# A fused attention and mixture-of-experts layer, its repeated step put into another order on all four engines

## The chip, the cores and the metric

One core of a Trainium2 chip runs the whole kernel. The metric is the device time of one execution in microseconds (us). A core has four compute engines with a queue each, worked through strictly in order: TensorE (PE in the profile, with PEld for its weight loads), VectorE (DVE), ScalarE (ACT) and GpSimd (POOL). SyncE (SP) issues transfers. Engines meet only at semaphores: an instruction that waits holds up everything behind it in its own queue.

## The reference

The input x has 16 sequences of 256 tokens with 128 features. Per token it is layer-normalised to xn, and the output is x plus an attention of xn plus a mixture of experts of xn:

```python
# attention, per sequence
x_tran  = xn @ W + b
weights = exp(tanh((x_tran @ xn.T) * (1 / |i - j|)))     # diagonal set to zero
attn    = (weights / (sum(weights, -1) + 1e-7)) @ xn
# experts: 8 of them, hidden size 176, each token takes its best 2
scores = sigmoid(xn @ gate_w.T); sel = top2(scores + expert_bias)
routed = sum over sel of relu((xn * score) @ w_up.T)**2 @ w_down.T      # bf16
shared = relu(xn @ shared_w_up.T)**2 @ shared_w_down.T                  # f32, hidden 176
y = x + attn + routed + shared
```

## The kernel before, in words

Two sequences make a chunk: 4 tiles of 128 tokens. There are 8 chunks (`NCH` = 8, `LAST` = 7). A chunk goes through three stages, and at each moment three chunks are under way: in iteration `k` of the repeated step, `f = k` is in its front, `c = k - 1` in its middle, `o = k - 2` in its end. The loop runs `k` = 3 to 7 (five steps). Chunks 0 to 2 are started by a list written out by hand before it, and a written-out tail follows it.

On TensorE the pieces are these functions, each with a line number that the profile shows:

- `transpose_x` (L877): the four tiles of xn are transposed into the PSUM bank `small`; ScalarE's `take_xT` (L418) copies them out as xnT.
- `rest` (L893): 64 output rows that hold the 8 gate logits and the last 48 shared hidden units. It writes `small` again, so it waits for `take_xT`. ScalarE reads it twice: `exp_logits` (L429), `relu_rest` (L434).
- `transpose_exp` (L902): the exponentials turned to one token per partition; it waits for both of these reads. VectorE's `route_one` (L641), `route_scores` (L650), `route_bias` (L659), `route_top` (L665), ScalarE's `take_pair`, VectorE's `route_mark` (L672) and GpSimd's `make_gates` (L287, L290) make the gates from it.
- `project` (L921) and `dots` (L936, for q = 0 and 1): xn W, copied by ScalarE's `take_proj` (L453), then its product with xn. VectorE's `weigh` (L686) multiplies by the decay, ScalarE does `take_tanh` and `take_exp` (L457, L462), GpSimd's `mask` (L309) clears the diagonal.
- `attend` (L957, q = 0 and 1): both write the bank `side`. So `attend(c, 1)` waits until ScalarE's `scale_attention` (L475) has read the first; that itself needs VectorE's `attend_sums` and `attend_norm` (L723, L727).
- `shared_main` (L970), `shared_down_rest` (L1011, with 64 rows of weights), `shared_down_main` (L1017): the shared expert. GpSimd squares its two hidden parts (`square_shared`, `square_rest`).
- `up_tile(c, t)` (L980, three matmuls, one per PSUM bank of `h_ps`) makes 1408 hidden values for each of 128 tokens. There is one such set of banks. VectorE's `gate(c, t)` (L698) reads it and multiplies by the gates; only when it has ended may the next `up_tile` start (semaphore `h_taken`). ScalarE's `square` (L505) follows, then SyncE turns the result by a transfer (L213), and `down_tile(c, t)` (L1029, eleven matmuls) takes it.

VectorE's `finish(c, h)` (L751) adds two tiles of the result, and SyncE stores them. `norm_stats` (L608, L616) on VectorE, then `rsqrt` and `normalize` (L263 to L276) on GpSimd make xn of a coming chunk, four tiles one after the other.

The order on every engine is only the order in which these calls are written. In the step before, TensorE runs up(c,0), attend(c,0), shared_down_rest(o), rest(f), up(c,1), shared_down_main(o), down(o,2), transpose_exp(f), attend(c,1), project(f), up(c,2), shared_main(c), dots(f,0), down(o,3), up(c,3), transpose_x(f+1), dots(f,1), down(c,0), down(c,1). The tail begins with `up_by_bank(0)` (L984 to L998), which is an `up_tile` of the last chunk whose two halves are gated separately, and waits in the same way for `gate(6, 3)`.

Of the kernel before, what the change touches and what calls it, by code (L numbers as in the profile page):

```python
# [12 lines left out]
P = 128  # L13
D = 128
# [17 lines left out]
def moe_attention_kernel(nc, x, early, late, up, down, out):  # L32
    NCH = x.shape[0]

    with ExitStack() as ctx:
# [129 lines left out]
        LAST = NCH - 1  # L165

# [83 lines left out]
        def _(pool):  # L250
# [127 lines left out]
            for k in range(3, NCH + 1):  # L378
                f, c = k, k - 1
                add_x(c)  # L380
                if f < NCH:
                    square_rest(f)
                if k + 1 < NCH:
                    rsqrt(k + 1)
                if k + 1 < NCH:
                    normalize(k + 1)
                if f < NCH:
                    make_gates(f)
                square_shared(c)
                if f < NCH:  # L390
                    mask(f, 0)
                if f < NCH:
                    mask(f, 1)
                if k + 1 < NCH:
                    narrow(k + 1)

        @block.scalar
        def _(act):
# [179 lines left out]
        def _(dve):  # L578
# [231 lines left out]
            finish(0, 0)  # L810
            gate(1, 3)
            finish(0, 1)
            weigh(2, 1)
            for k in range(3, NCH):
                f, c, o, g = k, k - 1, k - 2, k + 1
                gate(c, 0)
                attend_sums(c, 0)
                attend_norm(c, 0)
                if g < NCH:
                    norm_stats(g)  # L820
                gate(c, 1)
# [12 lines left out]
                finish(o, 1)  # L834
                weigh(f, 1)
# [21 lines left out]
        def _(pe):  # L857
            t_ = nc.tensor

            def transpose_x(c):  # L860
                if c == 0:
                    pe.wait_ge(ident_made, 1)
                if c == 1:
                    pe.wait_ge(rest_taken, 1)
                elif c == 2:
                    pe.wait_ge(expT_taken, 2)
                elif c > 2:
                    pe.wait_ge(proj_taken, c)
                for t in range(TILES):
                    if c == 0 and t < TILES - 1:  # L870
                        pe.wait_ge(first_xn_ready, t + 1)
                    elif c == 0:
                        pe.wait_ge(fourth_xn_ready, 1)
                    else:
                        pe.wait_ge(second_xn_ready, t - 1) if c == 1 and t > 1 else pe.wait_ge(xn_ready, xns(c, t))
                    bank, at = (dots_ps, t * P - S) if c == 0 and t >= 2 else (small, t * P)
                    last = t_.transpose(bank[:, at:at + P], xn[:, c, t, 0:D], ident[:, :])  # L877
                    if c == 0 and t == 1:
                        last.then_inc(first_half_made, 1)
# [310 lines left out]
```

## Time and profile before

| | before |
|---|---|
| median of 3 runs | 118.19 us (117.75 to 118.61) |
| the profiled execution, span from first to last instruction | 116.0 us |
| TensorE busy | 110.6 us (95%) |
| VectorE busy | 101.1 us (87%) |
| ScalarE busy | 89.5 us (77%) |
| GpSimd busy | 69.6 us (60%) |
| granted TensorE clock | 1.000 in every slice |

For the profiled execution only its span is given; the time of a run, as its median has it, is 2.2 us longer than that span, which lies around the first and the last instruction. In the profile a matmul of f32 operands is recorded as two instructions. Matmuls overlap: the time from the start of one piece to the start of the next is shorter than the duration shown. The chain of waits cuts the same stretch into pieces that add up.

### The profile page before, as it was taken

What the parts mean: (1) busy time and instruction counts of PE and PEld (TensorE: products, weight loads), DVE (VectorE), ACT (ScalarE), POOL (GpSimd) and SP (SyncE); (2) the same over time, 40 slices, a digit from 0 to 9 for tenths busy, and PEclk for the clock granted to TensorE, in tenths of its full rate; (3) what the DMA queues carried; (4) which work ended last, traced back from release to release, by engine and by line L of the source; (5) the groups of instructions that cost most, each with busy time, mean ns of one, the idle gap of its engine ahead of it and who ended that gap; (6) DMA issues with size and microseconds to landing.
All of it is one profiled execution on the core that took longest, in us unless ns stands there. A gap on an engine that the chain in (4) does not pass through costs nothing.

```text
span 116.0 us, 2804 instructions
## 1 busy us (share of the span) xinstructions
PE 110.6 (95%) x914; PEld 85.1 (73%) x914; DVE 101.1 (87%) x319; ACT 89.5 (77%) x139; POOL 69.6 (60%) x119
## 2 busy tenths in 40 slices
PE   3988999999999999999999999999999999999991
PEld 3965558787868776869578776879588767859790
DVE  6969989999998989989998989988998689989751
ACT  4444799987788987969799687969699687897760
POOL 6538993499999499635973499636972520613200
PEclk9999999999999999999999999999999999999999
DMA  4999105886776759892849939593949648687882
GB/s 97 319 263 331 68 0 100 78 167 126 139 145 108 195 100 193 54 245 48 167 82 220 124 70 179 103 163 79 172 84 219 124 84 164 117 216 136 131 208 90
DMA packets 47965, 16.56 MB, mean 143 GB/s; under 512 B 45008, under 2 KB 45904, under 8 KB 47952
## 3 DMA queue, kind: packets, MB, share of 16 engines
q1 hardware_dynamic: 47376, 15.44, 66.0%
q0 software_dynamic: 288, 0.72, 3.2%
q10 hardware_dynamic: 288, 0.23, 1.0%
q8 instruction: 7, 0.11, 0.4%
q14 instruction: 6, 0.05, 0.1%
HBM read 3.84 MB, written 2.10 MB: 51 GB/s over the span
## 4 chain that ended last, share of the span: by engine, by line
PE 94%; DVE 1%; issue 1%; POOL 1%; ACT 0%; DVEq 0%; POOLq 0%
PE out_ps L1029 16%; PE h_ps L980 15%; PE side L957 12%; PE dots L936 11%; PE out_ps L1017 6%; PE out_ps L1011 4%; PE small L921 4%; PE side L970 4%; PE small L893 4%; PE out_ps L1059 4%; PE small L877 3%; PE h_ps L993 2%; PE small L902 1%; PE side L912 1%; PE side L921 1%
## 5 line engine op out<-in xcount | busy, mean ns | idle before, releaser
L698 DVE SCALAR_TENSOR_TENSOR gated<-h_ps,gates 128x1408 bf16<-128x1408 f32 x28 | 45.2, 1615 | 4.7 <-PE h_ps L980 4.4
L505 ACT ACTIVATE hidden<-gated 128x1408 bf16<-128x1408 bf16 x30 | 41.1, 1378 | 2.6 <-DVE gated L698 1.6
L1029 PE MATMUL out_ps<-downT,hiddenT 128*128 128x128 bf16 x341 | 22.8, 219 | 0.0
L1029 PEld LDWEIGHTS out_ps<-downT,hiddenT 128*128 128x128 bf16 x341 | 20.8, 98 | 2.3 <-issue 0.6
L980 PE MATMUL h_ps<-upT,xnTb 128*128 128x512 bf16 (+1 forms) x84 | 21.3, 362 | 0.0
L276 POOL TENSOR_SCALAR xn<-x_sb,meanvar,rstd 128x128 f32<-128x128 f32 x26 | 20.4, 795 | 0.6
L957 PEld LDWEIGHTS side<-xn,probs 128*128 128x128 f32 x120 | 15.1, 191 | 1.5 <-issue 0.5
L957 PE MATMUL side<-xn,probs 128*128 128x129 f32 x120 | 15.8, 274 | 0.0
L936 PE MATMUL dots<-projT,xnT 128*128 128x256 f32 x60 | 15.4, 379 | 0.0
L309 POOL TENSOR_SCALAR_AFFINE_SELECT probs<-probs 128x256 f32<-128x256 f32 x16 | 6.5, 408 | 12.7 <-ACT probs L462 12.6
L980 PEld LDWEIGHTS h_ps<-upT,xnTb 128*128 128x128 bf16 x84 | 7.2, 98 | 9.4 <-issue 3.2
L936 PEld LDWEIGHTS dots<-projT,xnT 128*128 128x128 f32 x60 | 10.8, 190 | 3.9 <-issue 1.7
L457 ACT ACTIVATE weighted<-weighted 128x512 f32<-128x512 f32 x16 | 9.9, 620 | 1.9 <-DVE weighted L686 1.9
L686 DVE TENSOR_TENSOR weighted<-dots,decay 128x512 f32<-128x512 f32 x15 | 10.3, 684 | 0.4 <-PE dots L936 0.2
L321 POOL TENSOR_TENSOR resid<-scaled,x_sb 128x256 f32<-128x256 f32 x8 | 5.8, 729 | 7.5 <-ACT scaled L475 7.5
L315 POOL TENSOR_TENSOR shidden<-srelu 128x512 f32<-128x512 f32 x8 | 8.3, 1039 | 3.3 <-ACT srelu L467 3.3
L462 ACT ACTIVATE probs<-weighted 128x512 f32<-128x512 f32 x16 | 10.0, 625 | 0.3
L1017 PEld LDWEIGHTS out_ps<-late_sb,shidden 128*128 128x128 f32 x62 | 7.8, 191 | 1.0
L1017 PE MATMUL out_ps<-late_sb,shidden 128*128 128x128 f32 x62 | 8.4, 278 | 0.0
L271 POOL TENSOR_TENSOR rstd<-var_eps,minus_half 128x4 f32<-128x4 f32 x7 | 7.3, 1041 | 0.6
L713 DVE SCALAR_TENSOR_TENSOR gated<-h_ps,gates 128x704 bf16<-128x704 f32 x8 | 6.8, 886 | 0.5 <-PE h_ps L993 0.4
L429 ACT ACTIVATE expneg<-small,gate_sign 128x256 f32<-128x256 f32 x8 | 3.8, 474 | 4.4 <-PE small L893 4.3
(117 smaller groups left out, 178.9 us busy)
## 6 DMA issues: line engine op xcount, KB each, us to landing
x_sb<-in_x SPq DMA_DIRECT2D x7, 256.0 KB, 9.1
out_y<-final SPq DMA_DIRECT2D x7, 256.0 KB, 2.5
hiddenT<-hidden SPq DMA_TRANSPOSE x31, 3.6
upT<-in_up POOLq DMA_DIRECT2D x1, 352.0 KB, 7.5
downT<-in_down POOLq DMA_DIRECT2D x1, 352.0 KB, 8.4
late_sb<-in_late SPq DMA_DIRECT2D x1, 192.0 KB, 3.6
x_sb<-in_x ACTq DMA_DIRECT2D x1, 128.0 KB, 2.4
x_sb<-in_x SPq DMA_DIRECT2D x1, 128.0 KB, 2.5
```

The costliest lines, as they stand in the source:

```text
L276: g.tensor_scalar(xn[:, c, t, 0:D], x_sb[:, c, t, :], meanvar[:, c % 2, t, 0:1], rstd[:, c % 2, t:t + 1], ALU.subtract, ALU.mult).then_inc ...
L315: g.tensor_tensor(shidden[:, c % 2, :], srelu[:, c % 2, :], srelu[:, c % 2, :], ALU.mult).then_inc(sup_squared, 1)
L457: a.activation(weighted[:, c % 2, q, :], weighted[:, c % 2, q, :], ACT.Tanh).then_inc(tanh_done, 1)
L462: a.activation(probs[:, c % 2, q, :], weighted[:, c % 2, q, :], ACT.Exp).then_inc(exp_done, 1)
L505: a.activation(hidden[:, t, :], gated[:, t, :], ACT.Square).then_inc(squared, 1)
L686: v.tensor_tensor(weighted[:, c % 2, q, :], dots_bank(c, q), decay[:, :], ALU.mult).then_inc(dots_taken, 1)
L698: v.scalar_tensor_tensor(out=gated[:, t, :].rearrange("p (e h) -> p e h", e=E), in0=h_ps[:, 0:NH].rearrange("p (e h) -> p e h", e=E), scal ...
L936: last = t_.matmul(dots_bank(c, q)[:, k * S:(k + 1) * S], xnT[:, c % 4, at:at + P], projT[:, c % 2, q * S:(q + 1) * S], start=True, stop=True)
L957: last = t_.matmul(attend_bank(c, q)[:, t * (D + 1):(t + 1) * (D + 1)], probs[:, c % 2, q, k * S + t * P:k * S + (t + 1) * P], xn[:, c, 2 ...
L980: last = t_.matmul(h_ps[:, at:to], xnTb[:, c % 4, t * P:(t + 1) * P], upT[:, at:to], start=True, stop=True)
L1017: last = t_.matmul(out_at(c, t), shidden[:, c % 2, t * P:(t + 1) * P], sdown_main, start=False, stop=(t < 2 and c < LAST), skip_group_chec ...
L1029: last = t_.matmul(out_at(c, t), hiddenT[:, c % 2, t, j, :], downT[:, j, :], start=(t == 0 and j == 0 and c < LAST), stop=((t >= 2 or c == ...
```

## The change

No instruction of the loop is added or taken out; nearly all of them change place. On TensorE, `shared_down_rest` and `rest` of a step are moved to the end of the step before it, `rest` thereby one chunk ahead; the transposes of a chunk and of its exponentials are issued one at a time between the three banks of an `up_tile`; `project` and `dots(f, 0)` come before `down(o, 2)`. The last transpose of chunk 3, `shared_down_rest(1)` and `rest(3)` are in the list ahead of the loop. ScalarE, VectorE and GpSimd are given orders to match: `square(o, 3)` opens the next step, `take_proj` stands ahead of `scale_attention`, `norm_stats` runs one chunk further ahead and at the step's end, the routing stands in front of `gate(c, 1)`, `add_x` behind `normalize`. SyncE's program is unchanged. `DOWN_FIRST` moves the flag that clears an output bank to the product that is now first in it.

```diff
+        DOWN_FIRST = (0, LAST - 1)
...
             for k in range(3, NCH + 1):
                 f, c = k, k - 1
-                add_x(c)
                 if f < NCH:
                     square_rest(f)
                 if k + 1 < NCH:
                     rsqrt(k + 1)
-                if k + 1 < NCH:
                     normalize(k + 1)
+                add_x(c)
                 if f < NCH:
                     make_gates(f)
+                    mask(f, 0)
                 square_shared(c)
-                if f < NCH:
-                    mask(f, 0)
+                if k + 1 < NCH:
+                    narrow(k + 1)
                 if f < NCH:
                     mask(f, 1)
-                if k + 1 < NCH:
...
-            square(1, 3)
             take_exp(2, 1)
+            exp_logits(3)
+            relu_rest(3)
             for k in range(3, NCH):
-                f, c = k, k - 1
-                exp_logits(f)
-                relu_rest(f)
+                f, c, o = k, k - 1, k - 2
+                square(o, 3)
+                take_proj(f)
                 scale_attention(c)
                 square(c, 0)
+                take_pair(f)
                 square(c, 1)
-                take_proj(f)
-                take_pair(f)
+                take_tanh(f, 0)
+                take_exp(f, 0)
+                if f < LAST:
+                    take_xT(f + 1)
                 relu_shared(c)
                 square(c, 2)
-                take_tanh(f, 0)
-                if f + 1 < NCH:
-                    take_xT(f + 1)
-                take_exp(f, 0)
-                square(c, 3)
                 take_tanh(f, 1)
                 take_exp(f, 1)
+                if f < LAST:
+                    exp_logits(f + 1)
+                    relu_rest(f + 1)
+            square(LAST - 1, 3)
...
             finish(0, 0)
+            finish(0, 1)
             gate(1, 3)
-            finish(0, 1)
             weigh(2, 1)
+            norm_stats(4)
             for k in range(3, NCH):
-                f, c, o, g = k, k - 1, k - 2, k + 1
+                f, c, o, g = k, k - 1, k - 2, k + 2
+                route_one(f)
                 gate(c, 0)
                 attend_sums(c, 0)
                 attend_norm(c, 0)
+                route_scores(f)
+                route_bias(f)
+                route_top(f)
+                finish(o, 0)
+                gate(c, 1)
+                attend_sums(c, 1)
+                attend_norm(c, 1)
+                attend(c)
+                weigh(f, 0)
+                route_mark(f)
+                gate(c, 2)
+                finish(o, 1)
+                weigh(f, 1)
+                gate(c, 3)
                 if g < NCH:
                     norm_stats(g)
-                gate(c, 1)
-                route_one(f)
-                route_scores(f)
-                attend_sums(c, 1)
-                route_bias(f)
-                attend_norm(c, 1)
-                attend(c)
-                finish(o, 0)
-                route_top(f)
-                gate(c, 2)
-                weigh(f, 0)
-                route_mark(f)
-                gate(c, 3)
-                finish(o, 1)
-                weigh(f, 1)
...
+            def transpose_exp(c, i):
+                if i == 0:
+                    pe.wait_ge(logits_taken, c + 1)
+                    if c > 0:
+                        pe.wait_ge(rest_taken, c + 1)
+                made = t_.transpose(exp_bank(c)[:, i * P:(i + 1) * P], expneg[:, i * P:(i + 1) * P], ident[:, :])
+                if i == 1:
+                    made.then_inc(expT_made, 1)
...
+            def up_bank(c, t, bank):
+                if bank == 0:
+                    if c == 0 and t == 0:
+                        pe.wait_ge(up_cast, 16)
+                    if t == 0:
+                        pe.wait_ge(xTb_ready, c + 1)
+                    wait(pe, h_taken, TILES * c + t)
+                at, to = bank * CH, min((bank + 1) * CH, NH)
+                made = t_.matmul(h_ps[:, at:to], xnTb[:, c % 4, t * P:(t + 1) * P], upT[:, at:to],
+                                 start=True, stop=True)
+                if bank == 2:
+                    made.then_inc(h_made, 1)
+
             def up_tile(c, t):
+                for bank in range(3):
+                    up_bank(c, t, bank)
...
+                                  start=((i == 0 and (h == 1 or c not in DOWN_FIRST)) or (c == LAST and h == 1)),
...
             dots(1, 1)
-            transpose_x(2)
-            up_tile(0, 3)
+            transpose_tile(2, 0)
+            up_bank(0, 3, 0)
+            transpose_tile(2, 1)
+            up_bank(0, 3, 1)
+            transpose_tile(2, 2)
+            up_bank(0, 3, 2)
+            transpose_tile(2, 3)
             attend(0, 1)
...
             dots(2, 0)
+            transpose_tile(3, 0)
             down_tile(0, 2)
             down_tile(0, 3)
-            up_tile(1, 3)
-            transpose_x(3)
+            up_bank(1, 3, 0)
+            transpose_tile(3, 1)
+            up_bank(1, 3, 1)
+            transpose_tile(3, 2)
+            up_bank(1, 3, 2)
             dots(2, 1)
             shared_main(1)
+            transpose_tile(3, 3)
+            shared_down_rest(1)
+            rest(3)
             down_tile(1, 0)
             down_tile(1, 1)
             for k in range(3, NCH):
                 f, c, o = k, k - 1, k - 2
-                up_tile(c, 0)
+                up_bank(c, 0, 0)
+                transpose_exp(f, 0)
+                up_bank(c, 0, 1)
+                transpose_exp(f, 1)
+                up_bank(c, 0, 2)
                 attend(c, 0)
-                shared_down_rest(o)
-                rest(f)
+                project(f)
+                shared_down_main(o)
                 up_tile(c, 1)
-                shared_down_main(o)
+                attend(c, 1)
+                dots(f, 0)
+                if f < LAST:
+                    transpose_tile(f + 1, 0)
                 down_tile(o, 2)
-                transpose_exp(f)
-                attend(c, 1)
-                project(f)
-                up_tile(c, 2)
+                up_bank(c, 2, 0)
+                if f < LAST:
+                    transpose_tile(f + 1, 1)
+                up_bank(c, 2, 1)
+                if f < LAST:
+                    transpose_tile(f + 1, 2)
+                up_bank(c, 2, 2)
+                if f < LAST:
+                    transpose_tile(f + 1, 3)
+                down_tile(o, 3)
                 shared_main(c)
-                dots(f, 0)
-                down_tile(o, 3)
+                dots(f, 1)
                 up_tile(c, 3)
-                if f + 1 < NCH:
-                    transpose_x(f + 1)
-                dots(f, 1)
+                if f < LAST:
+                    shared_down_rest(c)
+                    rest(f + 1)
                 down_tile(c, 0)
                 down_tile(c, 1)
             c, o = LAST, LAST - 1
```

`transpose_tile(c, t)` is one pass of the former loop of `transpose_x(c)`, with the same waits. In the list ahead of the loop the transposes of exponentials 1 and 2 are likewise put between the banks of `up(0, 1)` and `up(1, 1)`.

## Rows read from the trace of the kernel before

**Rows 1.** the whole loop; us, then busy us of each engine and count, clock, DMA

```profile
36.07:100.39 64.32, 64.32 (x549) 49.11 (x547) 58.06 (x178) 53.53 (x81) 39.87 (x66) 1.00 0.73 136
```

**Rows 2.** the chain of waits in one step: start us, us, piece

```profile
62.14 0.59 PE h_ps L980 x3
62.73 0.89 PE side L957 x8
63.62 0.65 PE out_ps L1011 x8
64.27 0.58 PE small L893 x4
64.85 0.70 PE h_ps L980 x3
...
66.44 0.61 PE out_ps L1029 x11
67.06 0.22 PE small L902 x2
...
68.18 0.86 PE small L921 x2
...
70.49 0.86 PE dots L936 x4
...
72.56 0.44 PE small L877 x4
```

**Rows 3.** timeline of VectorE in that step: start us, us, line, instruction

```profile
62.77 1.62 DVE L698 SCALAR_TENSOR_TENSOR gated<-h_ps,gates 128x1408 bf16<-128x1408 f32 x1 [0.57 <-PE h_ps L980]
64.31 0.15 DVE L723 TENSOR_SCALAR rowsum<-side 128x2 f32<-128x2 f32 x1
...
68.21 0.16 DVE L723 TENSOR_SCALAR rowsum<-side 128x2 f32<-128x2 f32 x1 [0.32 <-PE side L957]
...
69.13 0.41 DVE L751 TENSOR_TENSOR final<-out_ps,resid 128x256 f32<-128x256 f32 x1
...
71.39 0.69 DVE L686 TENSOR_TENSOR weighted<-dots,decay 128x512 f32<-128x512 f32 x1
...
72.60 1.62 DVE L698 SCALAR_TENSOR_TENSOR gated<-h_ps,gates 128x1408 bf16<-128x1408 f32 x1
```

**Rows 4.** timeline of ScalarE in that step

```profile
64.90 0.47 ACT L429 ACTIVATE expneg<-small,gate_sign 128x256 f32<-128x256 f32 x1 [1.04 <-PE small L893]
65.27 0.38 ACT L434 ACTIVATE rest_relu<-small 128x256 f32<-128x256 f32 x1
65.53 0.63 ACT L475 ACTIVATE scaled<-side,rownorm 128x128 f32<-128x128 f32 x2
...
69.07 0.69 ACT L453 ACTIVATE projT<-small,early_sb 128x512 f32<-128x512 f32 x1 [0.31 <-PE small L921]
```

**Rows 5.** timelines of TensorE and ScalarE ahead of the loop, chunk 3

```profile
33.98 1.02 PE L970 MATMUL side<-xnT,late_sb 128*128 128x512 f32 x2
...
35.04 0.60 ACT L467 ACTIVATE srelu<-side 128x512 f32<-128x512 f32 x1
35.53 0.59 ACT L418 ACTIVATE xnT<-small 128x512 f32<-128x512 f32 x1
36.39 0.63 ACT L457 ACTIVATE weighted<-weighted 128x512 f32<-128x512 f32 x1 [0.26 <-DVE weighted L686]
```

**Rows 6.** timelines of VectorE and TensorE ahead of the loop, fourth tile of chunk 0

```profile
18.26 1.61 DVE L698 SCALAR_TENSOR_TENSOR gated<-h_ps,gates 128x1408 bf16<-128x1408 f32 x1
...
20.24 0.76 PE L980 MATMUL h_ps<-upT,xnTb 128*128 128x512 bf16 x3
```

**Rows 7.** timelines of VectorE and weight loads: a load that waited for a gate

```profile
13.04 1.62 DVE L698 SCALAR_TENSOR_TENSOR gated<-h_ps,gates 128x1408 bf16<-128x1408 f32 x1
...
14.72 0.52 PEld L980 LDWEIGHTS h_ps<-upT,xnTb 128*128 128x128 bf16 x3 [0.47 <-DVE gated L698]
```

**Rows 8.** route_bias, line 659: ns min, median and max

```profile
L659 DVE TENSOR_TENSOR biased<-scores,early_sb x7: 180/183/666, 20.2 to 94.2; 128x32 f32<-128x32 f32 x7
```

More of the change, by code:

```diff
@@ L858, in _, with transpose_tile @@
             t_ = nc.tensor
-            def transpose_x(c):
[L861 to L868, printed above, removed]
-                for t in range(TILES):
[L870 to L879, printed above, removed]
-                last.then_inc(xT_made, 1)
+            def transpose_tile(c, t):
+                if t == 0:
+                    if c == 0:
+                        pe.wait_ge(ident_made, 1)
+                    elif c == 1:
+                        pe.wait_ge(rest_taken, 1)
+                    elif c == 2:
+                        pe.wait_ge(expT_taken, 2)
+                    else:
+                        pe.wait_ge(proj_taken, c)
+                if c == 0 and t < TILES - 1:
+                    pe.wait_ge(first_xn_ready, t + 1)
+                elif c == 0:
+                    pe.wait_ge(fourth_xn_ready, 1)
+                elif c == 1 and t > 1:
+                    pe.wait_ge(second_xn_ready, t - 1)
+                else:
+                    pe.wait_ge(xn_ready, xns(c, t))
+                bank, at = (dots_ps, t * P - S) if c == 0 and t >= 2 else (small, t * P)
+                made = t_.transpose(bank[:, at:at + P], xn[:, c, t, 0:D], ident[:, :])
+                if c == 0 and t == 1:
+                    made.then_inc(first_half_made, 1)
+                elif t == TILES - 1:
+                    made.then_inc(xT_made, 1)
+            def transpose_x(c):
+                for t in range(TILES):
+                    transpose_tile(c, t)
             def turn_decay():
@@ L895, in rest @@
                 last.then_inc(rest_made, 1)
-            def transpose_exp(c):
-                pe.wait_ge(logits_taken, c + 1)
-                if c > 0:
-                    pe.wait_ge(rest_taken, c + 1)
-                for i in range(2):
-                    last = t_.transpose(exp_bank(c)[:, i * P:(i + 1) * P], expneg[:, i * P:(i + 1) * P], ident[:, :])
-                last.then_inc(expT_made, 1)
+            def transpose_exp(c, i):
[6 more added lines that the diff above has]
+                    made.then_inc(expT_made, 1)
             def project_first(half):
@@ L970, in shared_main @@
                 t_.matmul(shared_bank(c), supT, xnT[:, c % 4, :], start=True, stop=True).then_inc(sup_made, 1)
-            def up_tile(c, t):
-                if c == 0 and t == 0:
-                    pe.wait_ge(up_cast, 16)
-                if t == 0:
-                    pe.wait_ge(xTb_ready, c + 1)
-                wait(pe, h_taken, TILES * c + t)
-                for at in range(0, NH, CH):
-                    to = min(at + CH, NH)
-                    last = t_.matmul(h_ps[:, at:to], xnTb[:, c % 4, t * P:(t + 1) * P], upT[:, at:to],
-                                     start=True, stop=True)
-                last.then_inc(h_made, 1)
+            def up_bank(c, t, bank):
+                if bank == 0:
+                    if c == 0 and t == 0:
+                        pe.wait_ge(up_cast, 16)
+                    if t == 0:
+                        pe.wait_ge(xTb_ready, c + 1)
[5 more added lines that the diff above has]
+                    made.then_inc(h_made, 1)
+            def up_tile(c, t):
+                for bank in range(3):
+                    up_bank(c, t, bank)
             def up_by_bank(t):
@@ L1011, in shared_down_rest @@
                         t_.matmul(out_at(c, 2 * h + i), rest_hidden[rows, c % 4, i * P:(i + 1) * P],
-                                  sdown_tail[rows, :], start=((i == 0 and (h == 1 or c == LAST)) or (c == LAST and h == 1)), stop=False, skip_group_check=True)
+                                  sdown_tail[rows, :],
+                                  start=((i == 0 and (h == 1 or c not in DOWN_FIRST)) or (c == LAST and h == 1)),
+                                  stop=False, skip_group_check=True)
             def shared_down_main(c):
@@ L1073, in _ @@
             project(1)
-            up_tile(0, 1)
-            transpose_exp(1)
+            up_bank(0, 1, 0)
+            transpose_exp(1, 0)
+            up_bank(0, 1, 1)
+            transpose_exp(1, 1)
+            up_bank(0, 1, 2)
             shared_main(0)
```

13 lines of the change are left out of this document (8 added, 5 removed).

## The prediction

> **What bounds the kernel now.** I read the windows first, then the chain of waits, then the timelines. TensorE is busy for all 64.32 us of the loop [rows 1]: four steps of 12.95 us and a last one, without transposes, of 12.51. The chain stays on TensorE through loop and tail; a step is simply the sum of its pieces [rows 2]. VectorE works 58.06 of the 64.32, ScalarE 53.53, GpSimd 39.87 [rows 1]: all have slack, but VectorE little. So an order can gain nothing by shortening another engine's idle time. What it can do is make TensorE wait, and each such wait is added in full, since TensorE catches nothing up.
>
> **What the change does to TensorE's work.** The same pieces in another order, at the same prices: up 0.59, attend 0.89, down 0.61, project 0.86, dots 0.86, four transposes 0.44 (0.11 each), two transposes of exponentials 0.22, shared_down_rest 0.65, rest 0.58 [rows 2]. shared_main has project's shape (0.86), shared_down_main attend's (0.89). After the two products on part of the array the up tile stands with 0.70 for 0.59 [rows 2]: 0.11 for the switch, once per step before and after. Putting a transpose between two banks I cost at nothing: four in a row take 0.44 with their weight loads hidden, and a bank's longer stream hides one better. Bounds are in the rivals. The step thus stays at 12.95 unless a wait appears. I went through every wait with these prices. Positions below are counted from a step's first up.
>
> What one wait costs: a gate that began at 13.04 and took 1.62 let the held weight load start at 14.72, 0.06 after its end [rows 7]. The matmul can begin with the load or up to 0.20 later; I take 0.12 from release to matmul for all engines. An ordinary reader starts 0.03 to 0.04 after the piece it reads: up ends at 62.73, its gate starts at 62.77, so 0.79 after that up's first matmul [rows 2, 3], project to take_proj likewise [rows 2, 4].
>
> *Ahead of the loop, fourth up tile of chunk 0.* The gate it waits for ended at 19.87; the tile began at 20.24, behind four transposes [rows 6]. Three of these now come later, so its place is 19.91. The gate itself ends 0.04 later, because up(0,1) now holds two transposes. 19.91 + 0.12 = 20.03: **0.12** lost. The other interleaved tiles there have their gate in time.
>
> *rest(3).* It now stands behind shared_main(1), one transpose and shared_down_rest(1), and needs take_xT(3), which ScalarE runs behind relu_shared(1), the reader of shared_main(1). From the end of shared_main (33.98 + 1.02 = 35.00) relu starts after 0.04, take_xT after 0.53, and it ends after 1.12 [rows 5]. With 0.12, rest can start 1.24 later. TensorE is there, from the same end (which lies 0.16 behind the next start, by the overlap), after -0.16 + 0.11 + 0.09 + 0.65 = 0.69. Loss: **0.53**. Before, a whole up tile, attend and shared_down_rest lay between.
>
> *The exponentials' first transpose of step 3.* rest(3) starts at 36.24, the two down tiles follow, the step starts at 38.06 and the transpose is due at 38.27. It waits for relu_rest(3). ScalarE must first do tanh of dots(2,1) (start 36.39, now 36.51 by the 0.12 above), exp (the same 0.63, start 37.17), exp_logits (37.70) and relu_rest (38.07 to 38.45) [rows 4, 5]; consecutive instructions there start 0.1 before the last ends. With 0.12 it is 38.57: **0.30**. In later steps take_exp ends near 12.2 and relu_rest near 12.8, before the next step.
>
> *attend(c, 1), steps 3 to 6.* It needs scale_attention, now queued behind take_proj. From the end of project: take_proj starts at 0.03 and takes 0.69, scale_attention starts 0.12 before its end and takes 0.63 [rows 4], done at 1.23, attend at 1.35. TensorE is there after -0.16 + 0.89 + 0.59 = 1.32. **0.03** a step, 0.12 in four. With 0.20 for the release it would be 0.11 a step; with none, 0.
>
> *up(c, 3).* It waits for gate(c, 2). VectorE's queue from gate(c, 1) on: 1.54 to the next start, then sums, norm and attend 0.92 (68.21 to 69.13), then weigh and mark 1.21 (71.39 to 72.60), then gate(c, 2) for 1.62 [rows 3]. up(c,1) starts at 3.45, gate(c, 1) at 4.24, gate(c, 2) at 7.91 and ends at 9.53; up could run from 9.65. TensorE reaches it at 9.78 in steps 3 to 6: free, by 0.13. In step 7 there are no transposes; it arrives at 9.34, plus the 0.03 already waited: **0.28**.
>
> *The tail's first up.* In step 7 only two down tiles lie between up(7-1, 3) and up_by_bank(0), for dots, which stood there, has gone forward. The gate in between needs 0.79 + 1.62 + 0.12 = 2.53; TensorE offers 0.59 + 0.61 + 0.61 = 1.81. **0.72**. Before, dots' 0.86 made it 2.67. In steps 3 to 6 shared_down_rest and rest fill the gap (3.1), and the wait is hidden. After it the tail's order is unchanged and it shifts as a whole.
>
> The other moves cost nothing. The turned tiles: the last square of a chunk is done at 1.2 of the next step and its down tile is due at 7.4, well over a transfer; square(c, 1) ends at 7.3 and down(c, 1) is due at 12.3. SyncE's one queue has the same order and waits, and the store now goes before the fourth turn with time in hand. normalize(f+1) works from 2.1 to 5.2, ahead of the first transpose at 5.8; if it were later, the single transposes would wait in turn. The dots, masks, squares and resid are done 0.5 us or more ahead.
>
> VectorE's route_bias is the one instruction of unsure price. Of seven, the median took 0.183 us and one 0.666 [rows 8]; the long one ran beside GpSimd's add of L321, the others beside nothing longer than the small power of L271. Now it meets normalize. Bounds: nothing, or 0.48 late each time. VectorE has 0.13 spare before gate(c, 1) and 0.13 before up(c, 3), so 0.48 costs 0.22 a step. I take 0.27, the rest of the normalize instruction under way, which is hidden but for about **0.1** in step 3.
>
> The Trainium skill (SBUF — State Buffer, Who interferes with whom) says that a VectorE instruction with two SBUF inputs and a GpSimd one that reads SBUF exclude each other for a whole instruction; the long row agrees. By this rule each of four steps has the delay, by the row's median none.
>
> **Sum:** 0.12 + 0.53 + 0.30 + 0.12 + 0.28 + 0.72 + 0.1 = 2.2, less some rounding: 2.1. The profile's span would be 116.0 + 2.1 = 118.1, a run 118.19 + 2.1 = 120.3.
>
> **Rivals.** *Not slower: single transposes nearly free.* Place: inside the up tiles. If a transpose between two 512-column banks costs half of its 0.11, six in a step save 0.33; if the switch's 0.11 also goes, since a down tile now follows rest, 0.44 a step, 2.2 in five. That cancels the waits: 118.1, no change. From 0.2 us a step on, the result is within 1%. Against: four transposes take 0.11 each with loads already hidden, so what is left is their own stream. Chance 0.14.
>
> *Slower still: VectorE's route_bias is held.* If each is held by 0.48, 0.9 more instead of 0.1: 121.1. Chance 0.12. If GpSimd's four normalize instructions follow one another so closely that route_bias waits for all (until 5.2 instead of 3.4), gate(c, 1) starts 1.7 late. up(c, 2), due at 6.5, waits 1.15 for it and up(c, 3) another 0.4: 1.6 in four steps, 126.6. Against: in the trace no routing instruction is held over several. Chance 0.04. The rule of the skill page above speaks for the first of these.
>
> *The waits ahead of the loop fall away* (0.95 of the sum), because ScalarE or the gate is earlier than I place it: 119.3, within 1%. Chance 0.08.
>
> **Numbers.** The forecast (120.3, own range 119.4 to 121.2) has 0.59. The rivals have 0.14, 0.12, 0.04 and 0.08, a true gain 0.03. 1% (1.18 us) is about what a measurement can tell here. Faster 0.03: nothing in TensorE's work shrinks. Within 1%: the two rivals of that kind, 0.22. Slower: the forecast and the held bias, 0.75. The range reaches from the first rival, 118.2, to 121.9, above the held bias.
>
> **What would show it.** TensorE busy below the span in the loop, with idle time at line 893 (rest 3, 0.5 us, released by ScalarE's xnT), at the first transpose of exponentials (0.3, relu), before up(6, 3) (0.3) and up_by_bank(0) (0.7, both released by gate). Steps of chunks 3 to 5 at 12.95 to 13.05 us. route_bias at 0.18 or near 0.5. Wrong would be: steps shorter than 12.9, or a wait on a turned tile.

## The result: 2.6% slower

The median after is 120.96 us (120.20 to 121.26, 6 runs), beside 117.97 us (117.58 to 118.85, 6 runs) for the kernel before. The ratio is 1.026, 95% interval 1.023 to 1.030: 3.0 us more. The profiled executions span 119.4 us and 116.0 us, 3.4 us apart, at a granted clock of 1.00 (2.4 GHz) in both. The forecast was 120.3 us, range 118.2 to 121.9.

From the page of the kernel after: busy time by engine, and the shares of the chain that ended last.

```profile
PE 111.2 (93%) x899; PEld 85.3 (71%) x914; DVE 101.7 (85%) x319; ACT 89.0 (75%) x139; POOL 70.1 (59%) x119
...
PE 77%; DVE 8%; DMA 4%; issue 4%; ACT 3%; POOL 1%; DVEq 0%; POOLq 0%; ACTq 0%
```

Before, 94% of the chain was TensorE's. Now VectorE, ScalarE and a transfer have places on it: TensorE waits. (15 of its matmul records are missing in this trace, all of them banks of up tiles, ten of these a first bank ahead of a single transpose; so its busy time is read a little low.)

The window from project(3) to project(7), columns as in [rows 1]:

```profile
40.82:93.38 52.56, 52.14 (x434) 40.04 (x441) 47.02 (x141) 42.42 (x64) 34.27 (x55) 1.00 0.69 129
```

52.56 / 4 = 13.14 us a step, against 12.95 before. Each of the steps 3 to 6 has the same 13.14. The tail, from its first up to the end, is unchanged: 119.4 - 103.79 = 15.6, and 116.0 - 100.39 = 15.6.

The chain of waits of the kernel after (start us, us, piece), which answers to [rows 2] in its middle part:

```profile
15.85 1.62 DVE gated L700
...
20.21 5.15 DMA hiddenT<-hidden
25.41 0.79 PE out_ps L1047 x11
...
38.88 0.28 ACT rest_relu L433
39.17 0.14 issue
39.30 0.30 PE small L912
...
69.02 0.59 PE h_ps L991 x3
69.61 1.03 PE side L968 x8
70.64 0.86 PE dots L947 x4
...
73.77 0.91 PE side L981 x2
...
101.39 0.61 PE h_ps L991 x3
102.03 1.62 DVE gated L700
103.66 0.14 issue
103.79 0.75 PE h_ps L1009 x3
```

The reader sees two kinds of loss. Three times the chain leaves TensorE for other engines or a transfer: from 15.85 to 25.41, from 31.1 to 39.30 and from 102.03 to 103.79. And inside the step two pieces have grown: attend (`side` x8) from 0.89 to 1.03, shared_main (`side` x2) from 0.86 to 0.91.

TensorE's timeline, with the idle time before an instruction and its releaser in brackets:

```profile
25.41 0.79 PE L1047 MATMUL out_ps<-downT,hiddenT 128*128 128x128 bf16 x11 [0.62 <-DMA hiddenT<-hidden]
...
36.91 0.65 PE L903 MATMUL small<-xnT,early_sb 128*64 128x256 f32 x4 [0.42 <-ACT xnT L417]
...
39.30 0.30 PE L912 MATMUL small<-ident,expneg 128*128 128x128 f32 x1 [0.40 <-ACT rest_relu L433]
...
65.61 0.27 PE L912 MATMUL small<-ident,expneg 128*128 128x128 f32 x1
65.72 0.38 PE L991 MATMUL h_ps<-upT,xnTb 128*128 128x512 bf16 x1
...
66.21 1.05 PE L968 MATMUL side<-xn,probs 128*128 128x129 f32 x8
```

A piece is measured from its start to the next one's, as the modelled ends overlap: from the first transpose (65.61) to attend (66.21) are 0.60, for a bank of 0.21, a transpose of 0.11, a bank of 0.16 and a transpose of 0.11. The first bank, whose record is missing, stands ahead of them: 65.61 less the end of the down tile's place (64.78 + 0.61) leaves it 0.22. The three banks make 0.59 as before. Singly they cost what they cost in a row.

ScalarE's timeline, answering to [rows 5] and [rows 4]:

```profile
35.77 0.60 ACT L466 ACTIVATE srelu<-side 128x512 f32<-128x512 f32 x1
36.27 0.59 ACT L417 ACTIVATE xnT<-small 128x512 f32<-128x512 f32 x1
...
38.78 0.38 ACT L433 ACTIVATE rest_relu<-small 128x256 f32<-128x256 f32 x1
...
68.16 0.69 ACT L452 ACTIVATE projT<-small,early_sb 128x512 f32<-128x512 f32 x1 [1.64 <-PE small L932]
68.75 0.62 ACT L474 ACTIVATE scaled<-side,rownorm 128x128 f32<-128x128 f32 x2
```

take_xT ends at 36.86 and rest starts at 36.91; relu_rest ends at 39.16 and the transpose starts at 39.30; scale_attention ends at 69.37. The weight loads that these waits hold:

```profile
17.52 0.33 PEld L991 LDWEIGHTS h_ps<-upT,xnTb 128*128 128x128 bf16 x3 [0.40 <-DVE gated L700]
...
69.48 0.52 PEld L968 LDWEIGHTS side<-xn,probs 128*128 128x128 f32 x4 [0.31 <-issue]
...
73.55 0.30 PEld L981 LDWEIGHTS side<-xnT,late_sb 128*128 128x128 f32 x2
...
101.21 0.33 PEld L991 LDWEIGHTS h_ps<-upT,xnTb 128*128 128x128 bf16 x3 [0.23 <-DVE gated L700]
```

attend(c, 1)'s load starts at 69.48, 0.11 after scale_attention's end. Its place behind up(c, 1) was 69.44 (68.85 + 0.59). The first matmul starts at 69.51, beside the load, and the eight take 0.97 instead of 0.89 to the next piece (70.48). So 0.07 are wait, and 0.08 are put down to a first load of 0.19 that no stream hides; with rounding the two make the 0.14 of the chain.

VectorE's timeline, answering to [rows 3] and [rows 8], and GpSimd's beside it:

```profile
68.60 0.19 DVE L661 TENSOR_TENSOR biased<-scores,early_sb 128x32 f32<-128x32 f32 x1
...
99.54 1.62 DVE L700 SCALAR_TENSOR_TENSOR gated<-h_ps,gates 128x1408 bf16<-128x1408 f32 x1
```

```profile
67.51 3.14 POOL L277 TENSOR_SCALAR xn<-x_sb,meanvar,rstd 128x128 f32<-128x128 f32 x4
```

route_bias at 68.60 takes 0.19 in the middle of the four normalize instructions: nothing holds it.

### The profile page after: what moved, and what is told of

Same layout as the page of the kernel before. It is cut to its first block, busy times and chain, and to the rows that moved or that the text cites. A ratio compares the mean times of both kernels' runs of the same rounds, so it can differ in the third digit from the quotient of the medians.

```text
span 119.4 us, 2789 instructions
## 1 busy us (share of the span) xinstructions
PE 111.2 (93%) x899; PEld 85.3 (71%) x914; DVE 101.7 (85%) x319; ACT 89.0 (75%) x139; POOL 70.1 (59%) x119
## 4 chain that ended last, share of the span: by engine, by line
PE 77%; DVE 8%; DMA 4%; issue 4%; ACT 3%; POOL 1%; DVEq 0%; POOLq 0%; ACTq 0%
PE out_ps L1047 12%; PE side L968 10%; PE h_ps L991 10%; PE dots L947 8%; PE out_ps L1035 6%; PE small L932 4%; DMA hiddenT<-hidden 4%; DVE gated L700 4%; PE out_ps L1077 4%; PE side L981 4%; PE out_ps L1027 4%; PE small L903 3%; PE small L882 3%; PE small L912 2%; PE h_ps L1009 2%
## 5 line engine op out<-in xcount | busy, mean ns | idle before, releaser
L991 PE MATMUL h_ps<-upT,xnTb 128*128 128x512 bf16 (+1 forms) x71 | 20.4, 359 | 0.3 <-issue 0.2
L991 PEld LDWEIGHTS h_ps<-upT,xnTb 128*128 128x128 bf16 x84 | 8.0, 98 | 6.1 <-DVE gated L700 1.3
L452 ACT ACTIVATE projT<-small,early_sb 128x512 f32<-128x512 f32 x6 | 4.1, 687 | 8.4 <-PE small L932 8.4
L288 POOL TENSOR_SCALAR hot<-marked 128x32 f32<-128x32 f32 x7 | 2.1, 307 | 11.8 <-DVE marked L674 11.7
L882 PE MATMUL small<-ident,xn 128*128 128x128 f32 x30 | 7.9, 281 | 0.2
```

The costliest lines, as they stand in the source:

```text
L882: made = t_.transpose(bank[:, at:at + P], xn[:, c, t, 0:D], ident[:, :])
L991: made = t_.matmul(h_ps[:, at:to], xnTb[:, c % 4, t * P:(t + 1) * P], upT[:, at:to], start=True, stop=True)
```

## The experiments

"Step" below is the distance from project(c) to project(c + 1). The kernel before was run again beside each group of experiments, so its median differs a little (117.58 to 117.97). Intervals are 95%. A median's interval is some 0.5 to 0.9% wide on either side in the smaller sets, so effects under 0.5 us were read from the traces, and the times are only asked not to contradict.

**Transposes singly, alone.** The kernel before, with up(c, 3) cut into banks and the four transposes put singly behind them.

```diff
-                up_tile(c, 3)
-                if f + 1 < NCH:
-                    transpose_x(f + 1)
+                up_bank(c, 3, 0)
+                if f < LAST:
+                    transpose_tile(f + 1, 0)
...
+                up_bank(c, 3, 2)
+                if f < LAST:
+                    transpose_tile(f + 1, 2)
+                    transpose_tile(f + 1, 3)
```

> The kernel before with one part of the change alone: in steps 3 to 6 the four transposes of the next chunk stand one at a time between and behind the banks of up(c, 3) instead of in a row behind it; all else as before. Theory: a single transpose costs its own 0.11 us between two banks, as in a row: steps stay at 12.95, span 116.0, no change of a run's time. Rival (nearly free): up to 0.33 us less a step, 1.3 in four. Third: a weight load is exposed at each change between f32 and bf16, 0.05 us each, six in a step: 0.3 more a step, 1.2 in four.

117.27 us (10 runs) beside 117.78; ratio 0.997 (0.994 to 1.000). The steps are 12.95. TensorE's timeline:

```profile
24.97 0.79 PE L1041 MATMUL out_ps<-downT,hiddenT 128*128 128x128 bf16 x11 [0.96 <-DMA hiddenT<-hidden]
...
85.21 0.38 PE L987 MATMUL h_ps<-upT,xnTb 128*128 128x512 bf16 x1
85.42 0.27 PE L879 MATMUL small<-ident,xn 128*128 128x128 f32 x1
...
86.02 0.38 PE L879 MATMUL small<-ident,xn 128*128 128x128 f32 x2
86.24 1.03 PE L943 MATMUL dots<-projT,xnT 128*128 128x256 f32 x4
```

Up tile and four transposes take 86.24 - 85.21 = 1.03, that is 0.59 + 0.44. The rival of nearly free transposes falls. The wait at 24.97 was not expected: this is the order of before up to there, so the late tile that the kernel after also shows is not the change's doing alone. The profiled execution took 118.20, the longest of the ten; the others are 0.4 to 1.2 below it, so most of them can hardly have had such a wait.

**The kernel after, once more**, unchanged, to see which of its waits return.

> The changed kernel again, unchanged, for the moment at 20 to 25 us: in its first profile the second turned tile landed 5.2 us after its issue (4.2 in the kernel before) and down(0, 1) waited 0.77 us for it. If the order causes this, the landing is 5.2 again and the wait is 0.8; if it is a matter of one execution, it lies near 4.2 and the span is near 118.6. The median of the runs moved by 3.0 us where the profile moved by 3.4, which speaks for part of it being chance.

120.65 us; ratio 1.025 (1.018 to 1.031). The waits at rest(3) (0.42), at the transpose of exponentials (0.41) and before the tail (0.46) return, and the steps are 13.14. down(0, 1) waits only 0.16, not 0.78: its tile landed 4.5 us after its issue, not 5.2.

**scale_attention first.**

```diff
-                take_proj(f)
                 scale_attention(c)
+                take_proj(f)
                 square(c, 0)
```

> The changed kernel with scale_attention(c) ahead of take_proj(f) in the loop, nothing else. Theory: attend(c, 1) waits for scale_attention, which waits behind take_proj; that wait is the 0.14 us by which attend(c, 1) takes 1.03 in the chain instead of 0.89. With scale first it ends 0.3 us before attend(c, 1) is due, so steps 3 to 6 shrink from 13.14 to 13.00 us. In step 7 the 0.14 turns into a wait of up(6, 3) for its gate, which is only just hidden now. Gain 0.56 us in all: span near 118.8, about 120.4 a run. Rival: the attend is long because VectorE or the mask is late, or because the weight load behind bf16 up matmuls is always exposed; then nothing changes, 13.14 a step, span 119.4.

119.65 us beside 117.78; ratio 1.015 (1.009 to 1.022). ScalarE's and TensorE's timelines:

```profile
66.85 0.63 ACT L474 ACTIVATE scaled<-side,rownorm 128x128 f32<-128x128 f32 x2 [1.81 <-DVE rownorm L729]
67.37 0.69 ACT L452 ACTIVATE projT<-small,early_sb 128x512 f32<-128x512 f32 x1
```

```profile
67.37 0.76 PE L991 MATMUL h_ps<-upT,xnTb 128*128 128x512 bf16 x3
67.96 0.83 PE L968 MATMUL side<-xn,probs 128*128 128x129 f32 x6
```

attend follows up after 0.59, and the steps fall from 13.14 to 12.995. This one exchange on ScalarE is worth 0.14 a step, as expected; 0.05 is left. From project(7) to the tail's first up it is 10.41 as in the kernel after: there up(6, 3) waits for its gate instead. The trace thus accounts for 0.56 us. The median is 1.0 and 1.3 below those of the two sets of the kernel after; the rest may be the early turned tile, in time in this profile, but four executions don't settle it.

**One transpose between down(o, 3) and shared_main.**

```diff
-                    transpose_tile(f + 1, 3)
                 down_tile(o, 3)
+                if f < LAST:
+                    transpose_tile(f + 1, 3)
                 shared_main(c)
```

> The changed kernel with the fourth transpose of the next chunk behind down(o, 3) instead of ahead of it, so that it stands between down(o, 3) and shared_main(c). Theory: shared_main takes 0.91 instead of 0.86 in the chain because its f32 weight load (0.19 us long) has only a down matmul of 0.05 to hide behind; behind a transpose it is hidden: 0.05 less in steps 3 to 6, 0.2 in all, steps of 13.09. Rival: the 0.05 is a wait on a semaphore (attn_taken); then the step stays at 13.14.

120.26 us; ratio 1.020 (1.014 to 1.026). Steps 13.09, 0.05 less. TensorE's timeline:

```profile
72.25 0.78 PE L1047 MATMUL out_ps<-downT,hiddenT 128*128 128x128 bf16 x11
72.86 0.28 PE L882 MATMUL small<-ident,xn 128*128 128x128 f32 x1
72.98 1.02 PE L981 MATMUL side<-xnT,late_sb 128*128 128x512 f32 x2
73.84 1.03 PE L947 MATMUL dots<-projT,xnT 128*128 128x256 f32 x4
```

shared_main takes 0.86 again. Its 0.19 weight load is longer than the 56 ns of a down matmul that it runs beside; behind a transpose (0.11) most of it is hidden, behind the last down matmul 0.05 shows.

**The copy of chunk 3 earlier.** T(3, 3) ahead of dots(2, 1), and take_xT(3) ahead of square(1, 2), so that rest(3) doesn't wait.

```diff
+            transpose_tile(3, 3)
             dots(2, 1)
             shared_main(1)
-            transpose_tile(3, 3)
...
+            take_xT(3)
             square(1, 2)
             relu_shared(1)
-            take_xT(3)
```

> The changed kernel with the fourth transpose of chunk 3 ahead of dots(2, 1) and take_xT(3) ahead of square(1, 2) and relu_shared(1). Theory: the 0.48 us wait of rest(3) goes, but the transpose of exponentials of step 3 still stands at the end of ScalarE's tanh, exp, exp_logits, relu_rest, whose start is set by VectorE's weigh(2, 1), not by rest(3). So that wait grows from 0.35 to 0.83 and the span stays at 119.4 (gain 0.0, at most 0.1). Rival: two independent waits, gain 0.48, span 118.9.

120.68 us; ratio 1.025 (1.018 to 1.031). rest(3) no longer waits, and the transpose of exponentials starts 0.84 behind its place instead of 0.36 (the idle times in brackets, counted from modelled ends, are 0.68 and 0.40). project(2) to project(3) is 12.33 in both kernels: the second wait takes over what the first gives back.

**relu_rest(3) earlier.** exp_logits(3) and relu_rest(3) ahead of the tanh and exp of (2, 1).

```diff
+            exp_logits(3)
+            relu_rest(3)
             take_tanh(2, 1)
             take_exp(2, 1)
-            exp_logits(3)
-            relu_rest(3)
```

> The changed kernel with exp_logits(3) and relu_rest(3) ahead of take_tanh(2, 1) and take_exp(2, 1), nothing else. Theory: ScalarE stands idle until weigh(2, 1) anyway; the two reads then end near 38.4 instead of 39.16, and the transpose of exponentials of step 3 waits no longer: gain 0.35 us, span near 119.05; rest(3) still waits its 0.48. Rival: the mask of dots(2, 1), now about 0.8 us later, holds attend(2, 1) back and nothing is gained.

119.90 us; ratio 1.017 (1.011 to 1.024). project(2) to project(3) is 11.95, 0.38 less. ScalarE does relu_rest well ahead, and only rest(3) still waits, as the rows of ScalarE and then of TensorE show:

```profile
36.52 0.47 ACT L428 ACTIVATE expneg<-small,gate_sign 128x256 f32<-128x256 f32 x1 [0.75 <-PE small L903]
36.90 0.38 ACT L433 ACTIVATE rest_relu<-small 128x256 f32<-128x256 f32 x1
```

```profile
35.82 0.65 PE L903 MATMUL small<-xnT,early_sb 128*64 128x256 f32 x4 [0.42 <-ACT xnT L417]
```

With both edits (in the kernel with all of them, below) it is 11.46: 0.87 less, where the one alone gave 0 and the other 0.38. The waits are in series: removing the earlier one is worth nothing while the later one stands.

**The last step.** In step 7 alone dots(7, 1) goes behind up(6, 3), and mark and weigh behind the gates.

```diff
-                dots(f, 1)
+                if f < LAST:
+                    dots(f, 1)
                 up_tile(c, 3)
+                if f == LAST:
+                    dots(f, 1)
...
-                route_mark(f)
+                if f < LAST:
+                    route_mark(f)
                 gate(c, 2)
                 finish(o, 1)
-                weigh(f, 1)
+                if f < LAST:
+                    weigh(f, 1)
+                else:
+                    route_mark(f)
                 gate(c, 3)
+                if f == LAST:
+                    weigh(f, 1)
```

> The changed kernel; in step 7 alone dots(7, 1) stands behind up(6, 3) again, VectorE takes gate(6, 2) ahead of route_mark(7) and gate(6, 3) ahead of weigh(7, 1). Theory: the tail's first up waits for gate(6, 3), which can't start until up(6, 3), which can't start until gate(6, 2) has ended. gate(6, 2) then starts 0.5 us earlier, up(6, 3) after a wait of 0.36 that was none, and dots fills the gap behind it: the wait of 0.72 at the tail goes and the tail starts 0.37 us earlier, span near 119.0. Rival: the last gates are held by route_mark and weigh just as long and the tail's halves wait, gain 0.

120.99 us; ratio 1.027 (1.019 to 1.036): the times show nothing of 0.4 us. In the trace, project(7) to the tail's first up is 10.03 (93.49 to 103.52) instead of 10.41 (93.38 to 103.79). The tail's wait is gone, and up(6, 3) waits 0.35 for its gate instead.

**The tail's wait, added to the kernel before.** The kernel before with dots(7, 1) ahead of up(6, 3) in step 7 and nothing else.

```diff
+                if f == LAST:
+                    dots(f, 1)
                 up_tile(c, 3)
...
-                dots(f, 1)
+                if f < LAST:
+                    dots(f, 1)
```

> The kernel before with one exchange: in step 7 alone dots(7, 1) stands ahead of up(6, 3), as in the change. Theory: only the two down tiles then lie between up(6, 3) and the tail's first up, which waits for gate(6, 3): up(6, 3) starts 0.86 later, its gate ends at +0.79 + 1.62, and the tail starts 0.66 later than before: span 116.7 at the same start, time 0.6 to 0.7 us longer, up_by_bank(0) shown waiting 0.6 to 0.7 for the gate. Rival: the wait of 0.72 in the changed kernel comes from VectorE's new order; then nothing changes here.

119.04 us (7 runs) beside 117.58 (31 runs); ratio 1.011 (1.008 to 1.014), 1.3 us. TensorE's and VectorE's timelines:

```profile
97.48 1.10 PE L936 MATMUL dots<-projT,xnT 128*128 128x256 f32 x4 [0.26 <-DVE weighted L686]
98.42 0.76 PE L980 MATMUL h_ps<-upT,xnTb 128*128 128x512 bf16 x3
99.02 1.39 PE L1029 MATMUL out_ps<-downT,hiddenT 128*128 128x128 bf16 x22
100.99 0.75 PE L993 MATMUL h_ps<-upT,xnTb 128*128 128x512 bf16 x2 [0.58 <-DVE gated L698]
```

```profile
96.65 0.69 DVE L686 TENSOR_TENSOR weighted<-dots,decay 128x512 f32<-128x512 f32 x1
```

The tail's first up comes 7.72 after project(7), against 6.47 before: 1.25. The wait for the gate is 0.75 of it (from 99.02 + 1.22 for the two down tiles to 100.99), expected at 0.66. The other 0.5 is a second wait that the expectation left out: dots(7, 1) overwrites the tile that weigh(7, 0) reads until 97.34, which holds it 0.42, and it takes 0.94 instead of 0.86 (97.48 to 98.42). So a pair of dots set this close costs twice.

**All of these edits of the kernel after together** (scale_attention first, the copy of chunk 3 earlier, relu_rest(3) earlier, the last step, the transpose between); each has its diff above.

> All four edits of e1, e2a, e2b, e3 and e4 together in the changed kernel. Theory: steps 3 to 6 at 12.95 (4 x 0.19 gained), the two front waits gone (0.83), step 7 and the tail's start 0.5 earlier: 2.1 us, span near 117.3, about 118.9 a run, still slower than the kernel before by what is left (the late landing, up(0, 2) and up(0, 3) 0.2, step 7 0.4). Rival: the waits move elsewhere and less than 1 us is gained. It would beat the kernel before only if the pieces themselves were shorter, which no row shows.

119.49 us; ratio 1.010 (1.001 to 1.020). Steps are 12.95 and project(2) to project(3) is 11.46, but a wait of 1.34 for the turned tile of (6, 3) stands in the tail. ScalarE's timeline shows why:

```profile
101.00 0.63 ACT L456 ACTIVATE weighted<-weighted 128x512 f32<-128x512 f32 x1 [1.42 <-DVE weighted L688]
...
102.20 2.63 ACT L504 ACTIVATE hidden<-gated 128x1408 bf16<-128x1408 bf16 x2
```

The moved weigh holds tanh for 1.42, and square(6, 3) is queued behind it although its gate is done. That was my own edit's fault, of the kind studied here.

**The same with square(6, 3) ahead of that tanh.**

```diff
+                if f == LAST:
+                    square(c, 3)
                 take_tanh(f, 1)
                 take_exp(f, 1)
-            square(LAST - 1, 3)
```

> The kernel e5 with square(6, 3) ahead of take_tanh(7, 1) on ScalarE in step 7. In e5 weigh(7, 1) was moved back, tanh waited 1.4 us for it, square(6, 3) stood behind and its turned tile landed 1.5 us late: down(6, 3) waited 1.34. Theory: here that square runs 1.8 us earlier and the wait is gone: span 1.3 below e5's at the same start, near 116.5, time near 118.2, within 0.5% of the kernel before. Rival: the landing of 5.3 us instead of 3.6 comes from something else in the tail and the wait stays.

118.38 us (10 runs) beside 117.58 (31); ratio 1.007 (1.005 to 1.010): 0.9 us of the 3.0 are left. The wait in the tail is gone. From its trace: up(6, 3) starts at 98.67, 0.43 behind its place (97.33 + 0.91), and the 0.91 of shared_main is 0.05 more than before, for in step 7 no transpose stands ahead of it. The front up to project(2) is 0.26 longer than before when its tile lands in time (13.96 against 13.70 from project(1), read in the previous kernel). These make 0.74. Here the tile was late (14.63); in how many executions it was, the times don't tell, and that may be the rest.

**The early turned tile sheltered.** In the kernel before, and in the one with single transposes, shared_down_rest(0) goes ahead of down(0, 1), so that the tile has 0.65 longer to land.

```diff
+            shared_down_rest(0)
             down_tile(0, 1)
-            shared_down_rest(0)
```

> The kernel before with shared_down_rest(0) ahead of down(0, 1) in the list ahead of the loop, nothing else. The second turned tile landed after 4.2, 4.5 or 5.1 to 5.3 us in ten profiles, the last in four of them, whatever the order. Theory: where it is late, TensorE now does 0.65 us of other work first: 0.65 to 0.8 less; where it is not, shared_down_rest waits 0.15 for scale_second. On average 0.1 to 0.3 us less than before, at the edge of what can be told. Rival: lateness is rare in unprofiled runs; 0.1 us more.

> The kernel of e7 (before, with single transposes in steps 3 to 6) and the exchange of e9 together. e7 came out at 0.9971 of before, with 0.994 to 1.0004, while its steps were 12.95 us as before's. If that 0.3% is chance, this one equals e9; if single transposes do save something outside the profile's sight, it is 0.3% below e9. It is the candidate for a version faster than both kernels, by 0.2 to 0.5 us at most.

117.70 us and 117.68 us (12 runs each) beside 117.58 (31); ratios 1.001 (0.999 to 1.004) and 1.000 (0.997 to 1.002). Neither gains. In both profiled executions the tile landed after 4.0 and 3.9 us, so the shelter had nothing to shelter from, and project(1) to project(2) took 13.79, 0.09 more than 13.70. No version measured beats the kernel before clear of noise.

## Why the prediction was right, and where it fell short

The sign and the mechanism were right: nothing shrinks on TensorE, a few short waits are added, and it catches none of them up. The times moved 3.0, the forecast was 2.1. Part of that nearness is luck: 0.38 of the sum (up(6, 3) and route_bias) never came, and made up for part of what was missed elsewhere. By term, in us, measured in the profile after:

| term | forecast | measured |
|---|---|---|
| up(0, 3) | 0.12 | 0.03 |
| up(0, 2) | 0 | 0.17 |
| turned tile of (0, 1) | 0 | 0.78 here; 0.76 to 0.82 in 4 of 9 executions, 0.11 to 0.17 in the others |
| rest(3) | 0.53 | 0.48 |
| transpose of exponentials, step 3 | 0.30 | 0.35 |
| attend(c, 1) | 0.12 | 0.14 in each of 5 steps: 0.70 |
| shared_main | 0 | 0.05 in each of 5 steps: 0.25 |
| up(6, 3) | 0.28 | 0 |
| tail's first up | 0.72 | 0.72 |
| route_bias | 0.1 | 0 |

Without the tile the right column is 2.7, with it 3.5. From project(1) to the tail's first up the two profiles are 3.48 apart (89.92 and 86.44); the spans are only 3.4 apart since the kernel after began 0.08 earlier. With the mean of the nine tile waits, 0.43, the column is 3.1, beside 3.0 in the times. The nine are all the profiles of the new order of the front, one execution each.

**The three waits ahead of the loop and in the tail** came as worked out. rest(3) and the transposes wait for ScalarE's queue, and the tail for a gate whose cover, dots, had gone forward. Undone one by one they gave 0 (behind rest(3) stood the exponentials), 0.38 (their whole wait) and 0.38 (half of the tail's, as up(6, 3) then waited). One step of the working was at odds with its own rule: by an overlap of 0.1, exp would have started at 37.04 and the term been 0.17. The 37.17 that was taken stands, for in the trace exp starts 0.66 behind tanh (37.23 and 37.89).

**The step that failed is attend(c, 1): "0.03 a step, 0.12 in four".** The place and the cause were right; two sizes were not. The wait is 0.07: scale_attention ended 0.02 later than placed, and from its end to the matmul it is 0.14 (0.11 to the load) where I took 0.12. The larger part I left out: behind the wait the eight matmuls came to 0.97, 0.08 more, which I put down to their first load of 0.19. Not every held piece pays that: dots(7, 1) in the experiment with the kernel before paid 0.08, the transpose of exponentials 0.03, rest(3) and up(0, 2) 0.01 at most. The edit that removes the wait gave 0.14 a step, both parts at once. It happens in step 7 as well, which I left out; there its removal gains nothing, as up(6, 3) waits for its gate instead.

**shared_main was priced by its length in another neighbourhood.** "It has project's shape" is true, and so is the 0.86 behind a dots or a transpose. Behind a down tile it costs 0.91, which the experiment with a transpose between the two turned back.

**up(6, 3)** was to wait 0.28. Its gate ended at 101.16 and it started at 101.22, hardly later than TensorE was there: the 0.19 that step 7 had already lost, and a release of 0.06 where I had taken 0.12, had eaten the difference. A wait further back is not added to one further ahead on the same engine; it is paid from it.

**up(0, 3)** lost 0.03 of its 0.12: from the first transpose to attend it is 1.06 (19.89 to 20.95), before 1.04. **up(0, 2)** I had passed over with "the other interleaved tiles there have their gate in time": gate(0, 1) ended at 17.47 and the load started at 17.52, so from dots(1, 0) to up(0, 2) it is 1.03 (16.50 to 17.53) instead of 0.86. I had looked at the interleaved tiles only.

**The rivals.** Nearly free transposes: refuted. The held route_bias: refuted for this neighbour; all seven took 0.191 to 0.197 us, those of steps 3 to 6 (that at 68.60 among them) in the midst of normalize. The Trainium skill (SBUF — State Buffer, Who interferes with whom) has a VectorE instruction with two SBUF inputs and a GpSimd one that reads SBUF exclude each other; beside normalize the trace doesn't agree. Beside GpSimd's addition it does, and not only once. These are the rows of the long instruction of before [rows 8], of GpSimd and of VectorE:

```profile
28.98 0.72 POOL L321 TENSOR_TENSOR resid<-scaled,x_sb 128x256 f32<-128x256 f32 x1
29.09 0.67 DVE L659 TENSOR_TENSOR biased<-scores,early_sb 128x32 f32<-128x32 f32 x1
```

The same route_bias of chunk 2 took 0.65 to 0.68 in nine of the fourteen profiled executions, each time started 0.10 to 0.13 behind the addition's start. In the five with a late turned tile it began as the addition ended or later, and took 0.19 to 0.24. What sets addition and normalize apart (two tensors read instead of one, for instance) wasn't tried. The kernel after itself has the long one in its second profile (0.66), where the tile was in time, so the change did not remove it.

**Open.** Why a transposing transfer issued near 20.2 us sometimes lands late. It was after 3.9 to 4.5 us in nine of fourteen profiled executions and after 5.1 to 5.3 in five, in the old order once out of five (5.3, with the single transposes) and in the new one four times out of nine. Whether the new order makes it likelier is not settled by these; in time it is 3.9 to 4.2 in the old order and 4.5 in the new. One thing goes with it in all fourteen: a single packet of queue q8, which the page calls instruction. In the nine it ran 0.6 to 0.8 us after the tile's issue, in the five 3.1 to 3.2 after. Whether the one causes the other or both follow from a third wasn't tried. The medians moved by 0.4 less than the spans, which fits a wait that is in some executions only.

## What to carry to other kernels

In a step that one engine fills, sum its pieces, then look for each moved piece at its release and at what hides its first weight load; 0.14 us in each of four steps outweighed either of the two waits on ScalarE ahead of the loop. Before a piece is moved forward, ask what it covered where it stood: dots hid a gate of 1.62 us in the one step that has no other cover. Waits in series hide one another: undoing the earlier one alone showed nothing here, so look at the distance between two fixed points, not at the idle time of one row.

## What the runs showed beyond that

- Starting after a wait took TensorE 0.05 to 0.06 us from a VectorE gate's end to the load (17.47 to 17.52, 101.16 to 101.21). From ScalarE's end it took 0.05 too at rest(3) (36.86 to 36.91), but 0.11 behind relu_rest and scale_attention (39.16 to 39.27, 69.37 to 69.48); what makes the difference wasn't tried.
- A 128-column fp32 transpose put between two 512-column bf16 banks costs its 0.11 us and no more, in the kernel after and in the one with single transposes alone, and the granted clock stays at 1.00.
- The first copies make the start vary: project(0) began between 7.1 and 7.8 us. Profiled spans compare only from a common piece: the kernel with dots(7, 1) moved spans 116.6, 0.6 over before, but loses 1.25 between the same two pieces and 1.3 in the times.
